# Third expert layer: the high part of the activations times both parts of the weights in one product of 512 columns

## The reference, cut to what matters

```python
gate_w = softmax(gate); topk_w, topk_i = top_k(gate_w, 2)      # 8 experts, 2 for each token
h1 = relu(x @ W1[e] + b1[e])        # 256 -> 512
h2 = relu(h1 @ W2[e] + b2[e])       # 512 -> 512
out_e = h2 @ W3[e] + b3[e]          # 512 -> 256, the third expert layer
result = sum of out_e * weight over the token's two experts
```

## Time and profile before

| | us |
|---|---|
| median of 3 runs | 1211.88 (1210.73 to 1212.16) |
| the profiled execution | 1210.59 |
| its span | 1208.6 |
| PE busy / DVE busy / ACT busy / POOL busy | 1138.2 / 810.8 / 736.0 / 548.5 |
| mean granted TensorE clock | 0.98 of 2.4 GHz |

### The profile page before, as it was taken

One profiled execution on the slowest core, in us unless ns is written; L12 is line 12 of the kernel. 1 busy time (PEld: TensorE's weight loads), 2 busy tenths in 40 slices (PEclk: granted clock), 3 DMA queues, 4 the chain that ended last, 5 costly groups with the idle time before them and its releaser, 6 DMA issues.

```text
span 1208.6 us, 23487 instructions
## 1 busy us (share of the span) xinstructions
PE 1138.2 (94%) x7525; PEld 769.2 (64%) x7582; DVE 810.8 (67%) x2327; ACT 736.0 (61%) x1628; POOL 548.5 (45%) x877
## 2 busy tenths in 40 slices
PE   7899999999999999997988899789999999999978
PEld 3333433434334343342415899789999999999968
DVE  4888888788787887977753444245555555567747
ACT  2466667666676666764655656556666656666645
POOL 7314136485674856748453447445222232222220
PEclk9899999999999999998989899899999999999999
DMA  8565637458374583743725477965755675832636
GB/s 214 161 199 177 213 107 222 137 186 245 114 228 149 174 244 102 219 155 114 262 84 212 127 240 227 315 179 121 203 142 146 208 239 128 288 67 50 175 88 209
DMA packets 101616, 213.65 MB, mean 177 GB/s; under 512 B 10917, under 2 KB 71341, under 8 KB 93046
## 3 DMA queue, kind: packets, MB, share of 16 engines
q1 hardware_dynamic: 86038, 192.42, 49.6%
q0 software_dynamic: 14304, 18.69, 8.5%
q10 hardware_dynamic: 1152, 1.05, 0.4%
HBM read 239.28 MB, written 74.29 MB: 259 GB/s over the span
## 4 chain that ended last, share of the span: by engine, by line
PE 73%; POOL 7%; DMA 6%; issue 5%; DVE 4%; ACT 3%; SPq 1%; ACTq 0%; POOLq 0%; DVEq 0%
PE bank L1054 30%; PE bank L1124 9%; PE bank L1155 8%; PE bank L1136 7%; PE bank L1140 5%; PE bank L1100 4%; DMA x<-yout,rows 4%; PE bank L1173 2%; PE bank L1108 2%; POOL routed L1925 2%; DVE junk L1590 2%; POOL x L1935 1%; PE bank L1069 1%; PE bank L1213 1%; PE bank L1193 1%
## 5 line engine op out<-in xcount | busy, mean ns | idle before, releaser
L1590 DVE CUSTOM_DVE_ANT_0 junk<-bank,mneg 128x512 bf16<-128x512 f32 x512 | 336.4, 683 | 97.8 <-PE bank L1124 97.2
L1321 ACT ACTIVATE pt<-bank 128x512 f32<-128x512 f32 x512 | 302.0, 595 | 163.7 <-PE bank L1140 112.1
L1935 POOL DMA_INDIRECT x<-yout,rows x78 | 122.8, 1574 | 300.1 <-ACT yout L1400 247.8
L1054 PE MATMUL bank<-hid,w 128*128 128x256 f32 x1872 | 243.4, 287 | 6.6 <-DVE hid L1738 6.5
L1738 DVE TENSOR_TENSOR hid<-full,hid 128x256 fp32r<-128x256 f32 x312 | 133.8, 433 | 152.5 <-ACT full L1395 150.0
L1054 PEld LDWEIGHTS bank<-hid,w 128*128 128x128 f32 x1872 | 230.1, 191 | 8.2 <-issue 4.0
L1390 ACT ACTIVATE hid<-bank,biases 128x256 fp32r<-128x256 f32 x312 | 149.9, 480 | 106.9 <-PE bank L1054 97.3
L1140 PE MATMUL bank<-mneg,identb 128*128 128x512 bf16 x391 | 150.7, 385 | 0.0
L1395 ACT ACTIVATE full<-bank,biases 128x256 f32<-128x256 f32 x312 | 149.4, 479 | 1.5 <-DVE hid L1738 1.4
L1054 PE MATMUL bank<-w,hid 128*128 128x256 f32 x936 | 121.2, 283 | 4.6 <-DVE hid L1738 4.6
L1155 PE MATMUL bank<-pt,vaug 128*17 128x512 f32 x1024 | 122.8, 597 | 1.4 <-ACT pt L1321 0.7
(11 more groups left out here) (184 smaller groups left out, 1487.0 us busy)
## 6 DMA issues: line engine op xcount, KB each, us to landing
w<-split_weights SPq DMA_DIRECT2D x80, 1024.0 KB
w<-split_weights SPq DMA_DIRECT2D x40, 2048.0 KB
split_weights<-w_parts SPq DMA_DIRECT2D x64, 512.0 KB, 3.8
w_parts<-in_W SPq DMA_DIRECT2D x64, 256.0 KB, 4.6
split_parts<-parts SPq DMA_DIRECT2D x28, 384.0 KB, 2.6
rows<-routed SPq DMA_DIRECT2D x39, 258.0 KB, 3.4
stacks<-split_parts SPq DMA_DIRECT2D x36, 256.0 KB, 5.5
qst<-split_parts SPq DMA_DIRECT2D x24, 256.0 KB, 5.1
```

Source lines behind the costliest of these rows:

```text
L1054: product = T.matmul(ps, w[p], x[q], start=(k == 0 and n == 0), stop=(k == len(weights) - 1 and n == 2))
L1321: A.activation(pt[n % len(pt)][:, :], bank[3 + n % 2][:, :], ACT.Exp, scale=float(D) ** -0.5).then_inc(exped.sem, 1)
L1590: V.tensor_tensor_reduce(junk[n % 2][:, :], bank[n % 3][:, :], mneg[:, 0, st, :], 1.0, FLOOR, ALU.add, ALU.max, rowmax[gi % 2][:, hh, st:s ...
L1935: G.indirect_dma_start(x2_dram, bass.IndirectOffsetOnAxis(ap=rows[j % NS][:, tt, E + 1:E + 2].bitcast(U32), axis=0), yout[j % 2][:, tt], N ...
```

## The change

For each half `tt` of layer 3, the two products with the high part of the activations become one: its moving operand is both parts of the weights side by side (two ranges of 256 columns, `CW` apart), and its result goes to both halves of the bank, high by high to columns 0 to 255 and high by low to columns 256 to 511. The product of the low part of the activations is as before, into columns 0 to 255. For the first three `k` the wide product comes first, for the last one the narrow product does. VectorE now makes two additions for each half instead of one: the bias and columns 256 to 511 into `yout`, then columns 0 to 255 and `yout` into `yout`; the second waits for the first on a new semaphore. ScalarE and GpSimd wait for the second.

```diff
+    y_begun = signal("y_begun", of("layer3"))
...
-                products(ps[:, 0:E], [[x[:, k, tt * P:(tt + 1) * P] for x in hid2[j % 2]] for k in range(HT)],
-                         [weights_of(j, 2, k * E, (k + 1) * E) for k in range(HT)]).then_inc(multiplied[2].sem, 1)
+                tokens = slice(tt * P, (tt + 1) * P)
+                for k in range(HT):
+                    chunk, first = divmod(W_COLS[2][0] + k * E, CW)
+                    both = w[j % 2][:, chunk, :, first:first + E]
+
+                    def high_product():
+                        return T.matmul(ps[:, :].rearrange("p (n e) -> p n e", n=2), hid2[j % 2][0][:, k, tokens], both,
+                                        start=(k == 0), stop=(k == HT - 1))
+
+                    def low_product():
+                        return T.matmul(ps[:, 0:E], hid2[j % 2][1][:, k, tokens], both[:, 0], start=False, stop=False)
+
+                    if k + 1 < HT:
+                        high_product()
+                        low_product()
+                    else:
+                        low_product()
+                        high_product().then_inc(multiplied[2].sem, 1)
...
-                V.tensor_tensor(yout[j % 2][:, tt], bank[4 + outs_place[j, tt] % 2][:, 0:E], biases[j % NS][:, 2 * HT:],
-                                ALU.add).then_inc(y_biased.sem, 1)
+                y, ps = yout[j % 2][:, tt], bank[4 + outs_place[j, tt] % 2]
+                V.tensor_tensor(y, ps[:, E:2 * E], biases[j % NS][:, 2 * HT:], ALU.add).then_inc(y_begun.sem, 1)
+                dve.wait_ge(*y_begun.at((j, tt)))
+                V.tensor_tensor(y, ps[:, 0:E], y, ALU.add).then_inc(y_biased.sem, 1)
```

## The result

| | before | after |
|---|---|---|
| median | 1211.4 us (1207.91 to 1216.11, 20 runs) | 1214.91 us (1211.13 to 1219.53, 20 runs) |
| after / before | | 1.0033, 95% interval 1.0019 to 1.0047 |
| the profiled execution | 1210.59 us | 1213.31 us |
| its span | 1208.6 us | 1211.2 us |

The change makes the kernel slower by 0.33%, some 4 us. I had forecast 3.8 us less.

The account below looks back on a forecast made before the run. PE was taken to bound the kernel from 820 us on, never idle there. 4.1 us from late tiles plus 0.15 from tile 2 less 0.45 at the end made 3.8 less: 1206.8 us profiled, 1208.1 median; range 1205.3 to 1212.4.

Parts of the forecast that it names:

- The wide slot, 217 ns: On PE in layer 3, one 512-column product to the next takes 217 ns, taken from rows for 215 and 220.
- the saving of 75 ns a half and 4.1 us in all: On PE, a layer 3 half costs 1340 ns against 1415; 55 halves from 820 us on save 4.1 us.
- the second rival: Layer 3's product cost goes with the columns: no saving, only the end's addition, 1212.3 us; chance 0.08.
- the first rival: Each product has a fixed cost of 11 ns: wide slot 225, 44 ns saved a half, 1209.8 us; chance 0.22.
- The narrow slot kept at 117.9: On PE in layer 3, the remaining 256-column products keep today's slot of 117.9 ns.
- Low parts not late: VectorE's second addition, 0.45 us a half, is hidden before the end; PE never waits for low parts, costing nothing.
- The third rival: In tiles 29 to 37 VectorE's additions make low parts late, giving back 2.3 us, 1210.4 us; chance 0.05.
- The end, 0.45 us: After the last tile nothing covers the second addition; the chain over its first half grows by 0.45 us.
- Tiles up to 10: Except tile 2, early tiles gain nothing, since adds and gating set their pace; at most 1.5 us more gain.
- Loads hidden: On PE, weight loads lie largely beside products, since the 117.9 ns slot is shorter than one load's recorded 191 ns.
- The fourth rival: Loads are not hidden: four loads of 106 ns leave each half, 23 us saved, 1189 us; chance 0.02.
- The fifth: The wide product loses its pace: slower from a slot of 244 ns on, 1273 us at 430 ns; chance 0.04.

Follow-up runs that it names:

- The padded kernel: The changed kernel with six unused unit-matrix products filling PE's wait behind the last tile; ratio to the kernel before 1.0010 (0.9991 to 1.0029).
- the wide products together: The changed kernel with each half ordered w w w n n n n w (w wide, n narrow), plus six unit-matrix products after the last tile; ratio to before 1.0027.
- the kernel before with padding: The kernel before with unused unit-matrix products filling PE's waits: four behind the last tile's products, 0.9988 (0.9973 to 1.0004); in five gaps, 1.0001 (0.9988 to 1.0013).

## Why the prediction was wrong, step by step

1. **The wide slot, 217 ns: failed, and the saving of 75 ns a half and 4.1 us in all with it.** Measured: 234 ns. It was the outcome of the second rival (cost goes with the columns: no saving), to which I gave 0.08. Its mechanism, though, is not what the chip does: with products of one width the slot is 226.7, within 2 ns of the first rival's 225. (Its 11 ns should read 10, 117.9 less 107.5; that decides nothing.) What no case of mine had is that half of the 13 ns is lost again as soon as widths alternate, with the other engines done as well as in the kernel. The step that failed is "because these two rows are nearest in length and load": rows 6 and 7 are of other types, in rows of one width.
2. **The narrow slot kept at 117.9: right for the changed kernel**, 117 to 118 ns. As the price of what was there before it was a wrong reading: layer 3's own slots were 114 ns in the even tiles and 120 in the odd ones. The even tiles had less to give than I counted, the odd ones more, and over both the new form is worth nothing.
3. **Low parts not late: failed, small.** The third rival's place and mechanism: two waits of PE, 0.10 and 0.18 us, for low parts behind VectorE's longer queue, and the stretch from tile 14 to 38 longer by 0.6 us, against the 2.3 I gave it. With one addition it is not longer; with 12 products and two additions in these tiles it is, by 0.5 us (295.68). So the additions do it.
4. **The end, 0.45 us: about right in size at the full clock, wrong in its path.** 17.35 us with two additions stand against 16.85 to 17.4 with one. Two paths end close together there. I added to the one through the add and its landing; the other goes through VectorE's matrix work, behind both halves' additions, and sets the end in most kernels with two. That it lengthened PE's wait from 1.17 to 1.63 us I had not looked at. In 2 of the 6 profiles with that wait (1.62 or 1.63 us) the clock went to 1.2 GHz behind it, and the end cost 1.65 us more: 19.0 instead of 17.35. Both were executions of the changed kernel; in the three with 12 products and two additions it held. With 1.22 us or less it fell at this place in none. The padded kernel's profile has no half clock there, and its median in the same comparison was 3.4 us below the changed kernel's (1222.61 and 1226.03 us), more than the 1.65. But with the wide products together the padding was there too, and the ratio was 1.0027. So what it is worth is not settled.
5. **Tiles up to 10 "at nothing; at most 1.5 us more": only a gain was weighed; the loss there is likely but not shown.** I counted only what the products could gain there, never what a later or busier VectorE could lose, in a stretch where the adds and the gating set the pace. By the profiles the loss is 4.5 us between the means (154.7 and 159.1, each over executions that scatter by 5), or 3.5 without what the choice of executions adds. By the times it is less: the changed form in tiles 0 to 27 alone measured 1.0008, 1 us with an interval up to 3, and two additions in tiles 0 to 11 alone 1.0006. Both groups fluctuate with the landings, so this is an association over 14 profiles, and its cause is open.
6. **Loads hidden: right.** The fourth rival falls. The fifth too: two ranges cost nothing, and 512 columns keep their pace.

In sum, the saving of 4.1 us is not there because the slots give nothing back. That is shown. Of the 4.7 us that the change costs on average, the low parts make 0.5 to 0.6 and the end, from profile to profile, between nothing and 2. The 2 to 4 us that are left I can only put down to the early tiles, where no run shows them for certain.

**What stays open.** Why the landing at 787 to 790 us is longer with the change. That the add, later by an addition, meets more of the next weights' transfer, whose start hangs on layer 3's last product and not on the addition, is an argument that no run here tried. Nor does either half of the change show the early loss by itself for certain. Whether it takes both halves together is unsettled: alone, the wide product measured 0.9984 and 1.0005, the additions 1.0006 and 1.0031. What sets layer 3's slot at 114 ns in even tiles and 120 in odd ones is open as well. And no version ran that beats the kernel before beyond doubt: the lowest ratios are those of the wide product with one addition (0.9984, after 1.0005), which leaves a term of the sum out, and of the kernel before with padding (0.9988).

## What to carry to other kernels

Before you count on fewer, longer instructions, measure the slot in the very order in which they will stand: 13 ns a product were real in a row of equal products, half of that was left in alternation, and nothing in the kernel. And read the slot that you want to beat from the very products that go, not from a mean over layers: here 117.9 ns hid 114 and 120. Work moved from the busiest engine to a half idle one is free only where that engine's results have slack; look for the stretches where it sets the pace, and price a delay there, not only a gain. The Trainium skill's advice in VectorE: DVE Perf Modes, section Rules for kernel authors, to keep the number of VectorE's operations small, held here: of the 78 more, those of tiles 12 to 37 alone made the stretch from tile 14 to 38 0.5 us longer, in a kernel where VectorE is busy 69%.

## What the runs showed that I had not expected

- Products of 512 and 256 columns in alternation take 353.7 ns a pair, though in rows of their own they take 226.7 and 120.
- The same product of 256 columns has a slot of 114 ns in layer 3 of the even tiles and of 120 ns in the odd ones, with PE busy throughout (the kernel before, tiles 28 to 36).
- PE's wait of 1.63 us ahead of the same products was followed by the 1.2 GHz level in two executions and by none in four. A fall also came further on in two profiles without it (the wide product with one addition and the kernel before again), where the first 24 final products took 4.60 us, against the 3.11 that the next 24 took.
- One landing of the same add, at the same place of the work, took between 5.70 and 9.46 us in different executions (both of the kernel before with padding, once in one gap and once in five). The changed form's five lie within that, from 7.93 to 9.07 us.
- The same kernel takes 1211 us in some comparisons and 1222 us in others, under the same chip number too. Part of it shows in tiles 11 to 13: from tile 11's layer 2 to 38's are 332.1 to 332.6 us in the profiles of the one level and 336.9 to 340.0 in the six of the other, with 295.1 to 295.8 from tile 14 on in both.
